# Time mixing of a recurrent layer: plain fp32 low-rank and output products, the next turn's norm ahead of the last group norm, and bonus work off VectorE

## The reference

```python
xn = _ln(x, ln1_w, ln1_b)
sx = _token_shift(xn, state[:, i1])
xxx = jnp.tanh((xn + sx * maa_x) @ maa_w1).reshape(b, l, 5, 1, EXTRA_MAA)
xxx = jnp.matmul(xxx, maa_w2).reshape(b, l, 5, E)
x5 = xn[:, :, None] + sx[:, :, None] * (maa_stack + xxx)
w = jnp.exp(-jnp.exp(time_decay + jnp.tanh(x5[:, :, 1] @ decay_w1) @ decay_w2))
r = (x5[:, :, 3] @ Wr.T);  k = (x5[:, :, 0] @ Wk.T);  v = (x5[:, :, 2] @ Wv.T)
g = jax.nn.silu(x5[:, :, 4] @ Wg.T)
def step(s, rkvw):
    a = k_t[:, :, :, None] * v_t[:, :, None, :]
    out = jnp.einsum('bhk,bhkd->bhd', r_t, u * a + s)
    return (a + w_t[:, :, :, None] * s, out)
...
att = ((a4 - m) * jax.lax.rsqrt(var + EPS)).reshape(b, l, E) * gn_w + gn_b
x = x + att * g @ Wo.T
```

## Time and profile before

| | us |
|---|---|
| median of three runs | 3261.84 (3258.31 to 3264.69) |
| the profiled execution | 3263.58 |
| its span | 3261.4 |
| time mixing, to the end of the last residual | 939.8 |
| mean granted clock of TensorE | 0.966 of full |

### The profile page before, as it was taken

The page is one execution under the profiler, slowest core; times in us unless marked ns, Lnnn a source line. Parts: engine busy times, 40 slices in busy tenths (PEclk is TensorE's granted clock), DMA queues, the critical chain, the costliest instruction groups (busy, mean ns, idle before and its releaser), DMA issues.

```text
span 3261.4 us, 42208 instructions
## 1 busy us (share of the span) xinstructions
PE 3035.8 (93%) x15248; PEld 2419.6 (74%) x15248; DVE 1884.2 (58%) x2741; ACT 1214.1 (37%) x2604; POOL 559.6 (17%) x367
## 2 busy tenths in 40 slices
PE   5888898888869799999999999999999999999899
PEld 3545555455448688888888887878888888888787
DVE  5895985976967554444644446455444464444644
ACT  4224124123124344343533434334443453343432
POOL 3463544645610000000100001001000010000100
PEclk8898998998989899999999999999999999999999
DMA  3001000010022321111111110112101111111011
GB/s 117 17 10 38 7 22 22 7 39 5 1 105 78 141 75 49 38 52 35 52 36 51 35 51 33 58 53 77 51 35 51 35 52 36 51 35 42 21 50 58
DMA packets 54179, 148.65 MB, mean 46 GB/s; under 512 B 5936, under 2 KB 7472, under 8 KB 52848
## 3 DMA queue, kind: packets, MB, share of 16 engines
q1 hardware_dynamic: 51792, 144.45, 12.9%
q0 software_dynamic: 2304, 3.15, 0.5%
HBM read 131.85 MB, written 12.58 MB: 44 GB/s over the span
## 4 chain that ended last, share of the span: by engine, by line
PE 63%; DVE 2%; ACT 1%; issue 0%; DMA 0%; ACTq 0%; DVEq 0%
PE ca_ps L60 18%; PE ca_ps L62 18%; PE ca_ps L61 18%; PE ca_ps L1788 4%; PE ca_ps L1772 3%; PE ca_ps L1780 2%; PE ca_ps L1814 1%; DVE ca_stats L68 0%; DVE ca_xres L1549 0%; DVE ca_ctx_lo L1580 0%; DMA ca_xres<-in_ctxT 0%; DVE ca_wq_lo L1507 0%; ACT ca_sk L1465 0%; DVE ca_h_lo L1574 0%; ACT L1465 0%
## 5 line engine op out<-in xcount | busy, mean ns | idle before, releaser
L1549 DVE TENSOR_TENSOR ca_xres<-ca_xres,ca_ps 128x512 f32<-128x512 f32 x384 | 263.9, 687 | 243.9 <-PE ca_ps L62 239.0
L1336 ACT ACTIVATE ca_pr<-ca_ps,ca_nb 128x129 f32<-128x129 f32 x512 | 181.8, 368 | 511.0 <-DVE ca_nb L1532 510.9
L60 PE MATMUL ca_ps<-ca_h_hi,ca_wq_hi 128*128 128x512 f32 x768 | 312.6, 407 | 4.8 <-DVE ca_h_lo L1574 4.4
L569 DVE TENSOR_TENSOR_SCAN tm_xn<-tm_wd,tm_vb 128x512 f32<-128x512 f32 x256 | 298.5, 1208 | 8.9 <-DVE tm_vb L564 0.5
L62 PE MATMUL ca_ps<-ca_h_hi,ca_wq_lo 128*128 128x512 f32 x768 | 302.7, 394 | 0.0
L61 PE MATMUL ca_ps<-ca_h_lo,ca_wq_hi 128*128 128x512 f32 x768 | 300.4, 391 | 0.0
L60 PE MATMUL ca_ps<-ca_wv_hi,ca_ctx_hi 128*128 128x256 f32 x1024 | 297.9, 291 | 0.0
L62 PE MATMUL ca_ps<-ca_wv_hi,ca_ctx_lo 128*128 128x256 f32 x1024 | 287.5, 281 | 0.0
L61 PE MATMUL ca_ps<-ca_wv_lo,ca_ctx_hi 128*128 128x256 f32 x1024 | 287.2, 281 | 0.0
L1289 POOL TENSOR_TENSOR ca_dv<-ca_bvr 128x256 f32<-128x256 f32 x32 | 23.8, 743 | 1453.1 <-DVE ca_v L1517 1443.5
L60 PE MATMUL ca_ps<-ca_wo_hi,ca_ct_hi 128*128 128x512 f32 x640 | 253.5, 396 | 0.2 <-DVE ca_xres L1549 0.2
(11 more groups left out here) (248 smaller groups left out, 6627.7 us busy)
## 6 DMA issues: line engine op xcount, KB each, us to landing
ca_sq<-in_wq SPq DMA_DIRECT2D x49, 512.0 KB, 4.6
ca_so<-in_wo SPq DMA_DIRECT2D x48, 512.0 KB, 3.5
ca_sk<-in_wk SPq DMA_DIRECT2D x33, 512.0 KB, 5.8
ca_sv<-in_wv SPq DMA_DIRECT2D x32, 512.0 KB, 3.5
ca_bvr<-in_bvb SPq DMA_DIRECT2D x32, 256.0 KB, 3.8
tm_xq<-in_x SPq DMA_DIRECT2D x16, 256.0 KB, 2.7
tm_gg<-in_l0w SPq DMA_DIRECT2D x4, 1024.0 KB, 4.9
tm_rr<-in_x SPq DMA_DIRECT2D x4, 1024.0 KB, 5.3
```

Source lines behind the costliest of these rows:

```text
L60: pe.matmul(out, lhs[0], rhs[0], start=first, stop=False)
L569: v.tensor_tensor_scan(state[t % 2][:, d, :], wd[:, g].rearrange("p b t -> p (b t)"), pair[:, d, :], 0.0, ALU.mult, ALU.add).then_inc(scan ...
L1336: ins = act.activation(pr[hd][:, b, :], ps[:, BANK_SC + b // 2, o:o + KW], ACT.Exp, bias=nbs[hd][:, b:b + 1], scale=SCALE, accum_out=sms[h ...
L1549: v.tensor_tensor(xres[U.h][:, U.quad * 4 + b, :], xres[U.h][:, U.quad * 4 + b, :], ps[:, BANK_O + b % 2, :], ALU.add).then_inc(o_out, 1)
```

## The change

It rewrites `time_mix` alone; `channel_mix` and `cross_attend` are untouched.

- maa_w1, decay_w1 and Wo are no longer split; their products are plain fp32 (`lora`, `decay_in`, `output`), straight from `tm_xf` and `tm_vv`. The hi and lo copies of the first two mixed inputs and of the gated rows are gone, and with them the split of Wo in turn 0.
- u is folded into the head sum once (`tm_head_sum_u`, four scaled copies). GpSimd multiplies r and k (`receptance_key`) two steps ahead of a quarter, TensorE sums over a head, ScalarE copies the sum to `tm_ew`, GpSimd multiplies by v (`bonus`). The bonus is added by a second product with `centre` into the same bank (`centred`), for which ScalarE copies the attention sums to `tm_h5` (`attended`). `value_lo` and the low parts of the Tanh rows go to GpSimd.
- Gates come at steps 8f+3 and 8f+5 of their own quarter, all four within the loop.
- A turn is now a `body`, from the Wv product to the end of the scan. Between two bodies stands a `joint(q)`: the end of turn q interleaved with the front of turn q+1. Turn 0 starts with `opening`, turn 3 ends with `closing`.
- The residual rows have a tile of their own, `tm_xres`, loaded before the scan. In turn 0 it first carries Wg, so that one weight load comes earlier.

The core of the diff:

```diff
@@ time_mix, tiles @@
-        head_sum = sb("head_sum", [P, P])
+        head_sum_u = sb("head_sum_u", [P, EC, P])
-        w_hi = sb("w_hi", [P, 5, EC, E], FR)
-        w_lo = sb("w_lo", [P, 5, EC, E], FR)
-        lora1 = (sb("lora1_hi", [P, EC, 160], FR), sb("lora1_lo", [P, EC, 160], FR))
-        dec1 = (sb("dec1_hi", [P, EC, 64], FR), sb("dec1_lo", [P, EC, 64], FR))
+        w_hi = sb("w_hi", [P, 4, EC, E], FR)
+        w_lo = sb("w_lo", [P, 4, EC, E], FR)
+        wo = sb("wo", [P, EC, E])
+        lora1 = sb("lora1", [P, EC, 160])
+        dec1 = sb("dec1", [P, EC, 64])
+        xres = sb("xres", [P, 4, E])
-        xnT = [pj[0], pj[1], mx[0], mx[1]]
+        xnT = [mx[0], pj[0], pj[1], mx[0]]
+        gn = [pj[0], pj[0], pj[0], mx[1]]
@@ GpSimd @@
+            def receptance_key(q, f):
+                gp.wait_ge(f_free, q * 12 + (8 + f + 1))
+                if f == 0:
+                    gp.wait_ge(decay_full, q * 4 + 4)
+                else:
+                    gp.wait_ge(bonus_full, q * 4 + f)
+                if f >= 2:
+                    gp.wait_ge(cent_full, q * 4 + (f - 1))
+                gp.tensor_tensor(quad3(h5[:]), quad3(rr[:, f, :]), kk[:, f, :, 1:L + 1], ALU.mult).then_inc(rk_ready, 1)
+
+            def bonus(q, f):
+                gp.wait_ge(bonus_out, q * 4 + (f + 1))
+                gp.tensor_tensor(vv[:, f, :, 1:L + 1], quad3(ew[:]), vv[:, f, :, 1:L + 1], ALU.mult).then_inc(bonus_used, 1)
...
                 for t in range(STEPS):
...
+                    for f in range(EC):
+                        if t == 8 * f - 2:
+                            receptance_key(q, f)
+                        if t == 8 * f + 1:
+                            bonus(q, f)
@@ ScalarE @@
+            def attended(q, f):
+                act.wait_ge(rs_used, q * STEPS + 8 * (f + 1))
+                if f < 3:
+                    act.wait_ge(bonus_full, q * 4 + (f + 2))
+                act.activation(h5[:], mx[f % 2][:], ACT.Copy).then_inc(att_ready, 1)
...
+            def joint(q):
+                roots(q + 1)
+                attended(q, 3)
+                act.wait_ge(rs_ready, q * STEPS + STEPS)
+                for c in range(EC):
+                    normalised(q + 1, c)
+                square(q, 3)
+                deviation(q, 3)
+                front(q + 1, False)
@@ VectorE, loop over the 32 scan steps and what follows it @@
-                    if t == 0:
-                        bonus(0)
-                    if 1 <= t <= 3:
-                        value_lo(t)
-                    if t in (2, 3):
-                        bonus(t - 1)
-                    if t == 5:
-                        bonus(3)
                     for f in range(3):
-                        if t == 8 * f + 10:
-                            add_bonus(f)
                         if t == 8 * f + 14:
                             inverse(q, f)
-                        if t == 8 * f + 15:
+                        if t == 8 * f + 15 and f < 2:
                             gated(q, f)
-                        if t == 8 * f + 17:
-                            gated_lo(f)
+            def joint(q):
+                norm_stats(q + 1)
+                gated(q, 2)
+                v.wait_ge(rs_used, q * STEPS + (STEPS - 2))
+                norm_apply(q + 1)
+                v.wait_ge(rs_ready, q * STEPS + STEPS)
+                v.wait_ge(rs_used, q * STEPS + STEPS)
+                shift(q + 1)
+                inverse(q, 3)
+                gated(q, 3)
+                mix(q + 1, 1)
+                mix(q + 1, 2)
+                residual(q)
@@ TensorE @@
+            def lora(q, k, c):
+                pe.wait_ge(xf_ready, q * (4 * J) + (c + 1))
+                rows = (P, LORA)[k]
+                ins = pe.matmul(pj[k][0:rows, :], lora1[:, c, k * P:k * P + rows], xf[:, c, :], start=c == 0, stop=c == EC - 1)
+                if c == EC - 1:
+                    ins.then_inc(lora_full, 1)
...
+            def centred(q, f):
+                pe.wait_ge(att_ready, q * 4 + (f + 1))
+                pe.wait_ge(bonus_used, q * 4 + (f + 1))
+                pe.matmul(mx[f % 2][:], centre[:], h5[:], start=True, stop=False)
+                pe.matmul(mx[f % 2][:], centre[:], vv[:, f, :, 1:L + 1], start=False, stop=True).then_inc(cent_full, 1)
...
-                def output(c):
-                    pe.wait_ge(y_split_ready, q * 4 + (c + 1))
-                    for b in range(4):
-                        ins = mm3(pe, vb[:, b, :], (y_hi[:, c, b, :], y_lo[:, c, b, :]),
-                                  (w_hi[:, 4, c, :], w_lo[:, 4, c, :]), c == 0, c == EC - 1)
+            def output(q, c, b):
+                pe.wait_ge(y_ready, q * 8 + (2 * c + 2))
+                ins = pe.matmul(vb[:, b, :], vv[:, c, b, 1:L + 1], wo[:, c, :], start=c == 0, stop=c == EC - 1)
+                if c == EC - 1:
+                    ins.then_inc(wo_full, 1)
...
+            def joint(q):
+                n = q + 1
+                output(q, 1, 0)
+                pe.wait_ge(cent_out, q * 8 + 6)
+                transposes(n, 0)
+                pe.wait_ge(y_ready, q * 8 + 6)
+                transposes(n, 1)
+                pe.wait_ge(g_ready, q * 4 + 4)
+                transposes(n, 2)
+                pe.wait_ge(xn_ready, n * 4 + 1)
+                transposes(n, 3)
+                centred(q, 3)
+                pe.wait_ge(xn_ready, n * 4 + 3)
+                lora(n, 0, 0)
+                lora(n, 0, 1)
+                variance(q, 3)
+                lora(n, 0, 2)
+                lora(n, 1, 0)
+                lora(n, 0, 3)
+                lora(n, 1, 1)
+                unpacks(q, 3)
+                pe.wait_ge(lora_out, n * 3 + 1)
+                pe.wait_ge(xn_ready, n * 4 + 4)
+                mix(n, 1, 0)
+                lora(n, 1, 2)
+                pe.wait_ge(y_ready, q * 8 + 8)
+                mix(n, 1, 1)
+                lora(n, 1, 3)
+                mix(n, 1, 2)
+                decay_in(n, 0)
+                mix(n, 1, 3)
+                decay_in(n, 1)
+                mix(n, 2, 0)
+                decay_in(n, 2)
+                mix(n, 2, 1)
+                decay_in(n, 3)
+                output(q, 1, 1)
+                mix(n, 2, 2)
+                output(q, 1, 2)
+                output(q, 1, 3)
+                mix(n, 2, 3)
+                for c in (2, 3):
+                    for b in range(4):
+                        output(q, c, b)
```

## The result

| | before | changed | ratio, 95% interval |
|---|---|---|---|
| median of the runs, us | 3261.45 (3258.31 to 3264.69, 4 runs) | 3212.62 (3204.80 to 3213.94, 4 runs) | 0.9845 [0.9833, 0.9857] |
| profiled execution, us | 3263.58 | 3213.54 | |

The change gains 1.55%, some 49 us. The forecast was 3172, with a range from 3157 to 3202: the direction was right, the size was not, and the result lies outside the range.

What follows compares the result with a forecast made beforehand. VectorE's work was taken to bound the scan, a chain of waits the joint. Scan -28.0, its start 0, joints -54.3, opening -6.3 and closing -1.8 sum to -90.4 us: 3173.2 profiled, 3172 median, range 3157 to 3202.

Steps and rivals of the forecast that it cites:

- Scan: Four scans: twelve extra operations a turn leave VectorE's loop at 0.58 us each, 7.0 us a turn, -28.0 in all.
- VectorE idle ahead of its first multiplication of a pass, released by ScalarE's seed: Scan passes: a sign listed as showing the prediction wrong, VectorE waiting for ScalarE's seed; no size given.
- TensorE in the scan: Scan, per group of eight passes: TensorE's 27.5 us fit against VectorE's 27.9 + 2.2, at the full clock.
- Scan's start: First scan passes: a gain of 0.5 us a turn offset by a lower-clock slow pass; together 0, between -2 and +4.5.
- Joint: Last scan step to next first value product: 39.4 us against a mean of 57.5, TensorE the bound; -54.3 over three.
- Rival A: Joint stays a chain of hand-overs at the lower clock: 49.1 us each, saving 8.4, total 3201; chance 0.14.
- Opening: Start of turn 0: first value product near 49.4 instead of 55.71 us, -6.3, between 0 and -10.
- plain products cost double at the lower clock: Opening: reason given for its bound of 0, the chain to 35.2 us may end later.
- Closing: Behind the last turn's scan: 21.5 us instead of 23.3, -1.8, between -2.8 and 0.
- B: Scan: GpSimd's eight new products per scan stall VectorE 1.0 us each, giving back 32 us, total 3204; chance 0.07.
- C: Scan: TensorE at the lower clock becomes the bound, a scan of 172 instead of 124.3 us, total 3390; chance 0.03.
- D: Everywhere: another wait takes the place of what the moves remove, so the time stays the same; chance 0.01.

Runs made afterwards that it cites:

- e4: Changed kernel with bonus copy behind the next seed, half gate away from the unpacking, and the scan's four bonus products back on VectorE: 3193.34 us.
- e5: Changed kernel with bonus copy behind the next seed, half gate away from the unpacking, and ScalarE's gate behind the seed of step 9: 3173.54 us.
- e9: e5 with the second quarter's four output products together ahead of the transposes, instead of three of them between the joint's mixes: 3176.17 us.
- e8: e5 with six plain fp32 products, result unused, filling TensorE's idle time in the opening: 3171.25 us.
- e10: e5 with the joint's narrow plain products in groups of one shape where the order allows: 3172.84 us.
- e7: e5 with two more 128x512 GpSimd products per group, written to a tile nobody reads: 3176.27 us.

## Why the prediction was wrong, point by point

Time mixing ended at 888.85; before it was 939.8. The prediction names 851 for it, but its own sum gives 939.8 - 90.4 = 849.4, and its total comes to 3171.5 and not 3172: two slips of 1.6 and 0.5 us that change nothing below. By the steps of the prediction:

- **Scan: -28.0 forecast, +8.8 measured. This is the miss.** Each part of the term was right: twelve operations leave, each costs 0.58 (e4: 0.60), and without new waits the scans are 28.6 us shorter (e5). The step that failed is the sentence "the bonus copy sits ahead of the next seed of the scan, which has over 2 us to spare by then". The seed has that much to spare when its spread product is done. I never asked when the copy itself could start. It starts when TensorE has made the bonus product, behind an accumulation of 1.72 us: 2.6 us behind the spread product, and 0.5 us of copy on top. That is 3.1 us against 2.2 to spare, and cost 5.6 us in turn 1, of which 1.7 came only with the lower clock of the next point. The prediction's own sign for this case, "VectorE idle ahead of its first multiplication of a pass, released by ScalarE's seed", is what the trace showed.
- **TensorE in the scan.** "It fits with little to spare" was a sum over a group, 27.5 against 30.1 us. The sum was right, TensorE's 109 us of 117 bound nothing in e5. But a sum says nothing of a due time: steps 11 to 13 hold a half gate, the variance and a half gate, the unpacking follows at 14, and VectorE waits for it at 15. Cost 2.6 us in the scan of turn 1, and through the lower clock behind it the 1.7 more ahead of step 26.
- **Scan's start, 0 forecast.** The slow spell that I feared came: in the second pass of turn 1 the granted clock was 0.65 in the changed kernel and 0.54 in e5. In e5, where no seed is late, the first two passes still take 3.51 and 3.49 us, so by itself it costs nothing. In the changed kernel they take 3.52 and 4.25, and 0.68 of the second is the wait for the late seed. A second spell came behind the wait at step 23.
- **Joint: -54.3 forecast, -51.7 measured.** Right, for 40.3 us instead of 39.4, with TensorE the bound as laid out. The 39.4 were partly luck. No spell at the lower clock came (1.7 too much), no idle time (0.9), and the sixteen transposes take 2.0, not 3.5: I had misread. A transpose of 128 columns is one record, not two as said ahead of the prediction (16 x 4 turns are 64 records in the trace), so the 0.22 us there is the price of two. Against it, two steps' accumulations lie behind the last scan and I counted one (1.7 too little), the twelve narrow products took 0.98 to 1.05 instead of 0.86 (1.8 too little), full-size and packed ones beside them, which pay for the change of shape too, 1.0 more, and the variance and the unpacking 1.4 instead of 1.0. Rival A did not come, and e9 shows that it was further off than I thought.
- **Opening: -6.3 forecast, -3.4 measured.** 49.4 was forecast and 48.4 to 52.5 is what this opening gives; which of them, the clock decides (e8), so a hit or a miss by 3 us was a matter of luck here. The bound "plain products cost double at the lower clock" was the right one.
- **Closing: -1.8 forecast, -0.2 measured.** TensorE is busy for 20.73 us, not 18.2, and 1.5 of that is the same uncounted accumulation of step 30. Against it the waits were 2.4 us, where I had left 3.3.
- **Projections: nothing forecast, -4.5 measured**, half of it in turn 0 (56.2 instead of 58.6). No run isolates a cause.

The misses are 36.8 for the scan, 2.6 for the joints, 2.9 for the opening, 1.6 for the closing and -4.5 for the projections: 39.4 of the 40.3 between the two profiled executions' forecast and measured time (3173.2 and 3213.54). No rival held the miss in its number. A, B and C priced a resource (the clock, GpSimd's interference, TensorE's capacity) where the fault was an order in a queue. D, another wait in the place of the extras, is what happened in the scans; but I had stated it, with a chance of 0.01, for every stage at once and not stage by stage.

With the orders mended (e5, 3173.54) the kernel stands 1.5 us from the forecast, so the scan's term was that of the change as it could be, not as it was written. That the total comes so near is partly luck: in e5 the projections give 4.6 us that I had not forecast, and cover what the joints (2.6) and the closing (1.6) lack.

One wait of 1 to 2 us in each group of eight passes, which any moved hand-over between engines can bring, is 16 to 32 us over the four scans; with it the range would have reached 3218 at least and held the result.

## What to carry to other kernels

When an instruction that waits is put into an in-order queue, ask two questions: when is what it waits for given, counted behind everything that stands ahead of it on the giving engine; and who stands behind the waiting one. "It has time to spare" must be said of the instruction behind, from the instant at which the one ahead can start. And a capacity that fits over a group of steps can still miss a due time inside it: go step by step, with each hand-over's deadline.

## What was not expected of the hardware

- A plain fp32 product of 512 columns on a part of the array (32 rows, or 32 or 64 columns) takes 0.98 to 1.05 us from start to start between products of another shape, and 0.86 at full size. It is the change of shape that costs, 0.1 to 0.2 us each time; in a row of one shape the records are 0.43 apart, narrow or not (e10). In the joint of the changed kernel (TensorE, turn 1 to 2):

```profile
456.94 1.89 PE L664 MATMUL tm_pj<-tm_xf,tm_lora 128*128 128x512 f32 x4
...
464.27 1.12 PE L653 MATMUL tm_mx<-tm_h,tm_lora 32*128 32x512 f32 x2
465.32 1.04 PE L664 MATMUL tm_pj<-tm_xf,tm_lora 128*32 128x512 f32 x2
466.30 1.12 PE L653 MATMUL tm_mx<-tm_h,tm_lora 32*128 32x512 f32 x2
```

- VectorE's busy time in the scan of turn 1 moved by 0.01 us in 116 when GpSimd's work beside it grew by 9 us (e7).
- Six products whose result nobody reads brought the first value product forward by 4 us against e5, since the work behind them ran at the higher clock, 1.05 instead of 2.0 us a product (e8).
